# A five-step gated graph network on one core: order of the first loads, three more adjacency slots, and the symmetry test moved off TensorE

## The reference, cut to what matters

```python
# x: 2048x256 f32; A = adj: 2048x2048 int32 of zeros and ones (drawn symmetric, with ones on the diagonal)
Af, AfT = A.astype(f32), A.astype(f32).T
state = x
for _ in range(5):
    a_in  = Af  @ (state @ in_W.T + in_b)
    a_out = AfT @ (state @ out_W.T + out_b)
    a = concat([a_in, a_out, state])                 # 2048 x 768
    r = sigmoid(a @ r_W.T + r_b)
    z = sigmoid(a @ z_W.T + z_b)
    h = tanh(concat([a_in, a_out, r * state]) @ h_W.T + h_b)
    state = (1 - z) * state + z * h
out = tanh(state @ o1_W.T + o1_b) @ o2_W.T + o2_b
return layernorm(x + out)
```

## Time and profile before

| | us |
|---|---|
| median of the timed runs (lowest, highest) | 703.66 (703.58, 704.54) |
| the profiled execution | 703.13 |
| its span | 701.3 |
| TensorE (PE) busy | 684.9 |
| VectorE (DVE) busy | 469.9 |
| ScalarE (ACT) busy | 239.3 |
| GpSimd (POOL) busy | 50.0 |

### The profile page before, as it was taken

The page is one execution under the profiler, slowest core; times in us unless marked ns, Lnnn a source line. Parts: engine busy times, 40 slices in busy tenths (PEclk is TensorE's granted clock), DMA queues, the critical chain, the costliest instruction groups (busy, mean ns, idle before and its releaser), DMA issues.

```text
span 701.3 us, 8251 instructions
## 1 busy us (share of the span) xinstructions
PE 684.9 (98%) x3168; PEld 569.2 (81%) x3168; DVE 469.9 (67%) x775; ACT 239.3 (34%) x369; POOL 50.0 (7%) x42
## 2 busy tenths in 40 slices
PE   7999999999999999999999999999999999999993
PEld 6877888888888888888888888888888888888883
DVE  4777758776576768566676956455586558564866
ACT  2755645442031235113131421213143112123645
POOL 0022021100001010010101000000000000000052
PEclk9999999999999999999999999999999999999997
DMA  8873536000000000000000000000000000000003
GB/s 279 285 220 124 179 89 212 31 0 1 1 0 1 1 1 0 0 0 0 0 0 0 0 0 0 0 0 0 0 0 0 1 1 1 0 1 0 1 0 124
DMA packets 18462, 27.27 MB, mean 39 GB/s; under 512 B 1920, under 2 KB 9472, under 8 KB 18432
## 3 DMA queue, kind: packets, MB, share of 16 engines
q1 hardware_dynamic: 16912, 26.48, 11.5%
q10 hardware_dynamic: 1520, 0.40, 0.3%
HBM read 24.78 MB, written 2.10 MB: 38 GB/s over the span
## 4 chain that ended last, share of the span: by engine, by line
PE 92%; DVE 3%; DMA 2%; ACT 2%; issue 0%; ACTq 0%; SPq 0%
PE bank L435 40%; PE bank L380 16%; PE bank L378 16%; PE bank L379 16%; PE bank L407 2%; DMA stage<-in_adj_dram 2%; PE bank L518 2%; DMA a<-in_L_gnn_r_W_dram 1%; PE bank L530 1%; ACT a L782 1%; ACT ring L603 1%; DVE a L1090 1%; PE bank L387 0%; DVE ring L789 0%; DVE stats L1096 0%; DVE rows L789 0%
## 5 line engine op out<-in xcount | busy, mean ns | idle before, releaser
L435 PE MATMUL bank<-ring,rows 128*128 128x512 f32 x1280 | 295.6, 390 | 1.3 <-ACT ring L603 1.2
L435 PEld LDWEIGHTS bank<-ring,rows 128*128 128x128 f32 x1280 | 239.4, 188 | 51.8 <-ACT ring L603 2.0
L637 ACT ACTIVATE work<-work,bias 128x512 f32<-128x512 f32 x120 | 86.7, 725 | 285.5 <-DVE work L865 284.9
L865 DVE SCALAR_TENSOR_TENSOR work<-degree,deg_w,bank 128x512 f32<-128x512 uint16 x120 | 88.9, 744 | 109.2 <-PE bank L380 108.9
L378 PE MATMUL bank<-u_c,fold 128*128 128x512 f32 x240 | 96.3, 401 | 0.0
L794 DVE CAST ring<-a 128x1024 fp32r<-128x1024 uint8 x128 | 89.0, 704 | 10.6 <-PE bank L435 10.6
L380 PE MATMUL bank<-u_c,fold 128*128 128x512 f32 x240 | 93.8, 391 | 0.0
L379 PE MATMUL bank<-u_c,fold 128*128 128x512 f32 x240 | 93.7, 390 | 0.0
L380 PE MATMUL bank<-st_c,own 128*128 128x512 f32 x160 | 62.5, 390 | 0.0
L378 PE MATMUL bank<-st_c,own 128*128 128x512 f32 x160 | 62.3, 390 | 0.0
L379 PE MATMUL bank<-st_c,own 128*128 128x512 f32 x160 | 62.2, 389 | 0.0
(11 more groups left out here) (122 smaller groups left out, 719.2 us busy)
## 6 DMA issues: line engine op xcount, KB each, us to landing
stage<-in_adj_dram SPq DMA_DIRECT2D x28, 512.0 KB, 5.3
work<-in_x_dram SPq DMA_DIRECT2D x1, 2048.0 KB, 15.5
a<-in_adj_dram SPq DMA_DIRECT2D x3, 512.0 KB, 11.3
res<-in_x_dram SPq DMA_DIRECT2D x3, 512.0 KB, 6.7
out_dram<-a SPq DMA_DIRECT2D x3, 512.0 KB, 3.5
a<-in_L_gnn_r_W_dram SPq DMA_DIRECT2D x1, 768.0 KB, 6.7
a<-in_L_gnn_z_W_dram SPq DMA_DIRECT2D x1, 768.0 KB, 8.8
stateT<-in_L_gnn_h_W_dram SPq DMA_DIRECT2D x1, 768.0 KB, 10.0
```

The source lines that it names most:

```text
L435: last = nc.tensor.matmul(u_bank[2 * (c % 2) + d][:, :], rows[:, part, j, d * P:(d + 1) * P], ring[:, p % RING, jj, :], start=(j == 0 and ...
L637: nc.scalar.activation(gates[:, g, e, :], gates[:, g, e, :], ACT.Tanh if g == H else ACT.Sigmoid, bias=bias[:, g, e:e + 1]).then_inc(gate_ ...
L865: nc.vector.scalar_tensor_tensor(out=gates[:, g, e, :], in0=degree[:, c * CW:(c + 1) * CW], scalar=deg_w[:, g, e:e + 1], in1=g_bank[s % 3] ...
```

## The change

Loads: SP issues r_W, in_W, out_W, the broadcast in_b and out_b, z_W, h_W, o1_W, o2_W, the four bias vectors, x in four DMAs of 512 KB, and then the adjacency; o2_b comes behind the adjacency. ScalarE issues none. The raw h_W and the broadcast biases now lie in `res`, which held nothing before the residual's x was loaded.

Slots: the three tiles of `res` become slots for pairs 7, 8 and 9 (behind a wait for the degree weights and for "own" of gate H, which read what lay there), and from pair 10 on six slots are used in turn. The residual's x waits until their last pairs have been read.

Preparation: TensorE takes fold g right behind the transposes of gate g, and o ahead of the last fold; VectorE reads in an order of its own (`READ`), with the degree weights behind "own" 0 and 1 and three pieces of x behind ("o", 1); the fourth piece comes between its stores. A fold waits for its two copies one by one. ScalarE takes pair 0, two turned banks and pair 1 behind the last fold.

Test: VectorE transposes the 32x32 squares of the packed rows (four instructions of 128x1024 bytes, in step 3, between the pairs of chunk 2), SP moves the squares between partitions with 16 DMAs of 32 KB, and VectorE compares bytes with bytes in the last step between the pairs of chunks 1 and 2 (eight instructions of 128x512).

```diff
-        PREP = [(k, 0) for k in (0, 1, "own")]
+        PREP = []
         for g in range(NG):
-            PREP += [(k, g + 1) for k in (0, 1, "own")] if g + 1 < NG else []
+            PREP += [(0, g), (1, g), ("own", g)]
+            PREP += [("o", 0), ("o", 1)] if g == NG - 1 else []
             PREP += [("fold", g)]
-        PREP += [("o", 0), ("o", 1)]
-        ACT_AHEAD = {("fold", 1): [("x", 0), ("x", 1)], ("o", 1): [("pair", 0), ("pair", 1)]}
-        DVE_AHEAD = {("own", 0): [("degree", 0)], ("own", 1): [("degree", 1)], ("fold", 1): [("degree", 2), ("x", 0)],
-                     ("o", 1): [("x", 1), ("x", 2), ("x", 3)]}
+        READ = [(0, 0), (1, 0), ("own", 0), (0, 1), (1, 1), ("fold", 0), ("own", 1), (0, 2), (1, 2), ("fold", 1),
+                ("own", 2), ("o", 0), ("o", 1), ("fold", 2)]
+        ACT_AHEAD = {("fold", 1): [("x", 0)], ("o", 1): [("x", 1), ("x", 2)],
+                     ("fold", 2): [("pair", 0), ("turned", 0), ("turned", 1), ("pair", 1)]}
+        DVE_AHEAD = {("own", 0): [("degree", 0)], ("own", 1): [("degree", 1), ("degree", 2)],
+                     ("o", 1): [("x", 0), ("x", 1), ("x", 2)]}
...
+        IN_RES = len(staged)
+        staged += [res[:, c, :].bitcast(I32).rearrange("p (j w) -> p j w", j=2) for c in range(NC - 1)]
+        AGAIN = [*range(STAGES), *range(IN_RES, len(staged))]
...
-            return (q, 1) if late_q < 0 else (late_q % STAGES, late_q // STAGES + 2)
+            return (q, 1) if late_q < 0 else (AGAIN[late_q % len(AGAIN)], late_q // len(AGAIN) + 2)
...
+                    if q == IN_RES:
+                        sp.wait_ge(deg_w_ready, NG * DB)
+                        sp.wait_ge(prep_read, times_read(("own", NG - 1)))
...
+            for n in range(NQ):
+                sp.wait_ge(squares_turned, NQ)
+                for r in range(NQ):
+                    sp.dma_start(moved_u8[n * SQ:(n + 1) * SQ, r], turned_u8[r * SQ:(r + 1) * SQ, n].rearrange("p (g b) d -> p g b d", g=NPK))\
+                      .then_inc(squares_moved, 16)
...
-                    if last_step and c < NPK:
-                        check_turn(c * NC + s)
...
-                        pe.wait_ge(prep_read, N_PREP + m - 7)
+                        pe.wait_ge(prep_read, times_read(PREP[N_PREP + m - 8]))
...
+            def turn_squares(n):
+                if n == 0:
+                    dve.wait_ge(packed, N_PACKS)
+                nc.vector.transpose(turned_u8[:, n], blocks_u8[:, n]).then_inc(squares_turned, 1)
...
                 nc.vector.scalar_tensor_tensor(
-                    out=scratch.rearrange("p (b q) -> p b q", b=BC), in0=t_bank[:, :].rearrange("p (b q) -> p b q", b=BC),
-                    scalar=1.0, in1=cols_u8[:, n % NC * BC:(n % NC + 1) * BC, n // NC, :],
+                    out=scratch.rearrange("p (b d) -> p b d", d=SQ), in0=moved_u8[:, r, g], scalar=1.0,
+                    in1=cols_u8[:, :, g, r * SQ:(r + 1) * SQ],
                     op0=ALU.mult, op1=ALU.not_equal, accum_out=differ[:, n:n + 1]).then_inc(check_read, 1)
...
                         pack(i)
+                    elif 0 <= i - N_PACKS < NQ:
+                        turn_squares(i - N_PACKS)
+                    elif 0 <= i - FIRST_CHECK < NPK * NC:
+                        check(i - FIRST_CHECK)
```

More of the change, by code:

```diff
@@ L114, in fast_path @@
         early = stateT[:, :, :].rearrange("p d n -> p (d n)")
-        gate_raw = [g.rearrange("p (b k) -> p b k", b=DB) for g in (late[:, 0:NR], late[:, NR:2 * NR], early[:, 0:NR])]
+        gate_raw = [g.rearrange("p (b k) -> p b k", b=DB) for g in (late[:, 0:NR], late[:, NR:2 * NR], res.rearrange("p c w -> p (c w)")[:, 0:NR])]
         o_raw = late[:, 2 * NR:2 * NR + 2 * DB * D].rearrange("p (n b k) -> p n b k", n=2, b=DB)
[L117 to L122, removed]
+        gate_T = [g.rearrange("p (m d) -> p m d", d=D) for g in (early[:, 0:2 * DB * D], degree[:, :].bitcast(F32))]
+        lin_raw = early[:, 2 * DB * D:4 * DB * D].rearrange("p (n b k) -> p n b k", n=2, b=DB)
+        lin_bb = res.rearrange("p c w -> p (c w)")[:, NR:NR + 2 * D].rearrange("p (n d) -> p n d", n=2)
+        deg_scratch = res.rearrange("p c w -> p (c w)")[:, NR + 2 * D:NR + 4 * D]
         staged = [stage[:, n] for n in range(STAGES)]
@@ L286, in _ @@
                     slot, loads = slot_of(q)
+                    if q == IN_RES:
+                        sp.wait_ge(deg_w_ready, NG * DB)
+                        sp.wait_ge(prep_read, times_read(("own", NG - 1)))
                     if loads > 1:
-                        before = slot if loads == 2 else q - STAGES
+                        before = slot if loads == 2 else q - len(AGAIN)
                         sp.wait_ge(pair_ready, before + 1)
@@ L380, in three @@
                 return nc.tensor.matmul(out_, wl, vh, start=False, stop=last)
[L382 to L388, removed]
             def degrees(c):
@@ L648, in gate_chunk @@
                     degree_part(c)
+                if first and c == 0:
+                    act.wait_ge(b_loaded, 16 * (NG + 1))
                 for s in range(GATE):
@@ L713, in step @@
                 if first:
-                    for m in range(DB):
-                        turned_x(m)
-                    for m in range(2, NC):
-                        x_high(m)
                     for p in range(DB, NP):
@@ L741, in prepare @@
                             x_high(m)
+                        elif what == "turned":
+                            turned_x(m)
                         else:
@@ L753, in turned_x @@
                   .then_inc(x_read, 1)
-            for n, b in enumerate((in_b, out_b)):
-                act.dma_start(lin_bb[:, n], b.partition_broadcast(P)).then_inc(io_b_loaded, 16)
-            for n, b in ((R, r_b), (Z, z_b), (H, h_b), (NG, o1_b)):
-                act.dma_start(bias[:, n], b.rearrange("(b p) -> p b", p=P), allow_slow_non_contiguous=True)\
-                   .then_inc(b_loaded, 16)
-            act.dma_start(o2_bb[:, :], o2_b.partition_broadcast(P)).then_inc(o2_b_loaded, 16)
             prepare()
-            act.wait_ge(prep_read, N_PREP)
-            act.wait_ge(b_loaded, 16 * (NG + 1))
             step(0, first=True)
```

84 lines of the change are left out of this document (47 added, 37 removed).

## The result

The changed kernel takes 694.92 us (median of four runs, 694.74 to 695.94), the kernel before in the same comparison 703.62 us (703.09 to 704.54). The ratio is 0.9878, with a 95% interval of 0.9866 to 0.989: 8.7 us faster.

The account below looks back on a forecast made before the run. TensorE, busy 684.9 of 701.3 us, was taken as the bound. Terms -3.78 (test), -1.75 (holes) and -0.2 (start) gave -5.7, 703.1 to 697.4; plus 0.5 for the median, 697.9 us, range 696.6 to 700.3.

Parts of the forecast that it names:

- The test: Gates of chunks 1 and 2, last step: eight check_turns leave TensorE, -3.78 us, with VectorE's added work hidden.
- rivals 2 and 3: VectorE's byte transposes, step 3, chunk 2, take 1.5 to 2.5 us (time 700, chance 0.07) or 4.8 (708.6, 0.03).
- Rival 4: Last step's gates: another wait sets their pace, so only half the 3.78 us comes; time 699.8, chance 0.05.
- The holes: First two aggregations: three more slots close TensorE's waits for adjacency tiles, -1.75 us, ends 0 and -2.05.
- The preparation's own length: TensorE before the first aggregation: 20.55 us plus 0.2 for restarts, 20.75; order of instructions alone gains nothing.
- The hole that I expected at fold 1: Preparation: fold 1 waits for VectorE's copies, a TensorE hole of some 0.3 us.
- The tie with VectorE's list: End of preparation: VectorE's 13.4 us list ends at 27.7, TensorE's own work at 27.9.
- Rival 1: Start: VectorE's list or bias vectors ahead of x delay the first aggregation 1 to 2 us; time 699.9, chance 0.15.
- The start: Before the first transposes: r_W, no longer sharing with ScalarE's loads, lands earlier, -0.2 us.
- the end of -0.9: Best end for the start: r_W lands 0.7 us earlier and there is no hole at fold 1.
- The base: Whole kernel: the median of timed runs lies 0.5 us above the profiled execution, added to 697.4 for the forecast.

Follow-up runs that it names:

- b2: The kernel before with only the three tiles of res added as further adjacency slots: 701.00 us, ratio 0.9962.
- f1: The changed kernel without the extra slots and with the old symmetry test, so the start alone: 699.79 us, ratio 0.9946 to the kernel before.
- f2: The start alone, but with ScalarE issuing in_b, out_b and the four bias vectors as before the change: 702.27 us, ratio 0.9984 to the kernel before.
- after_third: The changed kernel itself, run again in a further comparison: 695.05 us, ratio 0.9876 to the kernel before.
- e1: The changed kernel with broadcasts behind z_W, bias vectors behind the seventh adjacency tile, degree weight 0 behind own 1, turned banks before pair 0: 696.12 us.
- a2: The changed kernel with only the two broadcasts (in_b, out_b) issued by ScalarE at the start: 697.51 us, ratio 0.9919 to the kernel before.
- b1: The kernel before with ScalarE issuing its seven small loads only when r_W has landed: 703.38 us, ratio 0.9998.
- b5: The kernel before with SP issuing ScalarE's seven small loads, order of work otherwise as before: 704.13 us, ratio 0.9992.
- after_again: The changed kernel itself, run again for scatter and a second trace: 695.09 us, ratio 0.9868 to the kernel before.
- a1: The changed kernel with ScalarE issuing in_b, out_b and the four bias vectors at the start: 697.20 us, ratio 0.99 to the kernel before.
- e2: The changed kernel with broadcasts behind z_W, bias vectors behind the seventh adjacency tile, turned banks before pair 0, degree weight 0 behind own 0: 694.41 us.
- d1: The kernel before with twelve warm-up products instead of seven: 703.53 us, ratio 0.9995.

## Why the prediction was wrong

By its own steps:

- **The test, -3.78: right.** 16.32 us against 18.21 in the stretch, in the whole change and alone. VectorE's transposes took 1.238 us of busy time, at a pitch of 1.16 with the cast behind it. Here is VectorE's timeline in the changed kernel:

```profile
460.54 1.24 DVE L857 STREAM_TRANSPOSE stage<-stage 128x1024 uint8<-128x1024 uint8 x1
461.70 0.65 DVE L824 CAST ring<-a 128x1024 fp32r<-128x1024 uint8 x1
```

  The forecast was 1.15, so rivals 2 and 3 fall, and aggregate 2 of step 3 has no hole (14.53 us for 64 matmuls, against 14.51). Rival 4 falls with the 16.32. The Trainium skill's page "Vector Engine (DVE) Microarchitecture Reference" has one element per cycle per lane for it, in its section on the reshape front-end, by which the prediction's estimate was 1.07 us; the trace has 0.09 more by the pitch, so the measured 1.16 stands. One reading in this step was wrong: the row at 493.48 lies in chunk 3 of step 3, and the transposes run in chunk 2, from 460.5 on. VectorE's lead over TensorE is the same there: pair 4 starts 4.59 us behind the aggregation's start, as in chunk 3, so the margin came out unchanged, by luck.
- **The holes, -1.75: right in size, only half right in cause.** 30.91 to 29.17 us, and ScalarE's waits for tiles fell from 8.0 us to one of 1.8. The slots alone do it (b2). So does the new order alone (f1, f2), because VectorE's first store comes earlier, which I had not followed from the edit of its list to SP's eighth load. On top of the start the slots bring 1.0 us, at 84 us, where I had named nothing.
- **The preparation's own length: right by luck.** I had 20.75 us from the first transpose to the first aggregation; after_third has 25.88 - 5.10 = 20.78. But the 20.75 had the slow first transposes of before in it (4.35 us for 24, where after_third has 2.13 and 1.53 for 12 each), and after_third has a wait of 0.98 us for z_W that I had not foreseen; the two cancel. The hole that I expected at fold 1 (0.3 us) is 0.1: the fold took 3.72 us and not 3.62. The tie with VectorE's list did not decide, but e1 shows how near it is: one degree weight moved makes a wait of 1.0 us there. Rival 1 falls with it: the start is earlier than forecast, not later.
- **The start, -0.2: this is the step that failed.** The words were: "Alone, r_W can land up to 0.26 MB / 0.35 = 0.7 us earlier; most of these bytes moved late, so I take 0.2." It landed 2.4 us earlier (6.75 to 4.3 from its issue), and even the end of -0.9 was too near. I had priced ScalarE's loads by their bytes at the queue's usual rate. a2 shows that the two broadcasts alone make r_W land 2.2 us later than in the changed kernel, three times the 0.7. Nor did they move late: in the profile of before in_b landed 5.2 us behind its issue at 0.75 and out_b 6.6 behind 1.22, so at 5.9 and 7.8, on both sides of r_W's 7.5, and from 2 to 4 us all 16 engines together moved only 39 and 85 GB/s. The profile of before had the evidence: a 768 KB load took 6.75 us where 0.35 MB/us asks for 2.2. The page's 0.3% of 16 engines' span, from which I took it that the adjacency would land as before, says how long packets were counted busy, not how long a load beside them waits.
- **That it comes through, too, was not worked out.** An earlier r_W is worth nothing in the old order (b1, b5: 0.9998 and 0.9992). It counts because fold 0 now follows the first 12 transposes and needs only in_W and out_W, which land close behind r_W (the one wait for them, in after_again, is 0.8 us). I wrote that the order of these instructions "alone gains nothing". f2's median of 1.1 us is not far from that, and I did not price the two together. What the lower clock costs behind a late r_W (up to 1.5 us, a1 against a2) was in no term either.
- **The base, +0.5: it did not carry over.** The profiled execution of before, 703.13, did lie 0.5 us under the median of its runs. But that distance is part of their scatter, and the changed kernel has less of it: 703.13 - 7.98 = 695.15 is its median (694.92 to 695.09) without anything added. The runs of before scatter from 702.15 to 706.43 over the four later comparisons, those of the changed kernel only from 694.80 to 695.46 in two. The early part varies from run to run (b2: clock at half, and the first aggregation 2.5 us later than in before), which an early r_W seems to remove; that this is the cause of the whole scatter was not shown.

By a usual run of after: -3.78 - 1.74 - 2.4 = -7.9 us, against 7.98 by the last matmul. The forecast had 5.7: of the 3.0 us that it missed 2.2 are the start, 0.5 the base, and 0.3 are unexplained.

## What to carry to other kernels

Price a load that runs beside the first load on the critical path by how late that load lands beside it and what the windows show meanwhile, not by its bytes at the queue's best rate: here 256 KB of one-row broadcasts cost 2.2 us instead of 0.7. An earlier landing and an order that can use it are worth 0 and 1.1 us apart and 3.6 us together, so price such edits as a pair and ask at each step what the engine does next with what is there. When an edit reorders an engine's list, follow its first store to the load that waits for that slot; the holes that more slots were to close may close without them and open elsewhere.

## What the runs showed of the hardware

- Broadcasts of one row to 128 partitions, two of 128 KB, pull the rate of all 16 DMA engines down wherever they stand in the queue. How far differs between executions: the lowest window is 53, 59 and 46 GB/s in the three profiles of the changed kernel and 165 in e2. In e1, where they follow z_W, the windows put the dip at 8 to 9 us:

```profile
6.00:7.00 1.00, 1.00 (x7) 1.00 1.03 393
...
8.00:9.00 1.00, 1.00 (x6) 1.00 0.96 55
```

- A 128x1024 transpose of bytes on VectorE in 32x32 squares costs 1.238 us of busy time at a pitch of 1.16, and 16 moves of 32 KB within SBUF behind it were issued in 10.1 us by SP and landed 1.8 us after issue each.
- TensorE's clock at the start differs between executions of nearly the same work: at 2.4 GHz from 10.68 on in the profile of before, and in b2 from 5.65 to 9.06, then at 1.2 GHz to 15.89. With the new order and a late r_W the upper level begins at 12.82 in a1 and at 5.72 in a2, and the first aggregation at 28.83 and 27.33. Filling the idle time ahead of r_W (d1) changed nothing in the median of the old order; in the new one it wasn't tried.
